# Moving work inside the fourth attention of a fused decoder: bias, residual, statistics, exponentials, two dense steps and the top-p weights

## The reference

```
x = x + tanh(g_xattn[l]) * xattn_l(layernorm(x), ctx)
x = x + tanh(g_ffn[l])   * ffn_l(layernorm(x))
```

```
q = _qdq(x) @ _qdq(wq).T + bq                 # rounded to whole numbers of a scale per token
attn = softmax(q k^T / sqrt(16))              # 16 heads of 16 features, 128 keys per sequence
o = attn v
out = _qdq(o) @ _qdq(wp).T + bp
```

## Time and profile before

| | us |
|---|---|
| median of 3 runs | 1033.53 |
| lowest, highest | 1028.81, 1034.68 |
| the profiled execution | 1037.46 |
| its span | 1035.6 |
| PE busy in the span | 859.2 (83%) |
| DVE, ACT, POOL busy | 677.9, 521.2, 326.0 |

### The profile page before, as it was taken

The page is one execution under the profiler, slowest core; times in us unless marked ns, Lnnn a source line. Parts: engine busy times, 40 slices in busy tenths (PEclk is TensorE's granted clock), DMA queues, the critical chain, the costliest instruction groups (busy, mean ns, idle before and its releaser), DMA issues. The chain is left out here.

```text
span 1035.6 us, 17165 instructions
## 1 busy us (share of the span) xinstructions
PE 859.2 (83%) x6369; PEld 532.9 (51%) x6369; DVE 677.9 (65%) x1402; ACT 521.2 (50%) x840; POOL 326.0 (31%) x267
## 2 busy tenths in 40 slices
PE   5978999776227776797979998778799999999997
PEld 3434665463216564574545554445455556555554
DVE  7985888787817667266336479645778657744343
ACT  4714345445117767336558743455456786533332
POOL 2531343312744555303025662100355333200000
PEclk9988999988659999897879999999999999999999
DMA  8973433310246677331013453111256445433332
GB/s 267 324 254 107 129 107 114 93 33 1 114 151 189 211 225 218 117 113 46 18 32 122 123 170 106 46 32 47 70 174 182 129 129 167 144 105 95 107 94 85
DMA packets 60191, 129.12 MB, mean 125 GB/s; under 512 B 9267, under 2 KB 25025, under 8 KB 60114
## 3 DMA queue, kind: packets, MB, share of 16 engines
q1 hardware_dynamic: 55506, 119.17, 37.4%
q0 software_dynamic: 4608, 8.94, 2.3%
HBM read 83.95 MB, written 48.27 MB: 128 GB/s over the span
## 5 line engine op out<-in xcount | busy, mean ns | idle before, releaser
L1448 PE MATMUL ps<-turned_buf,W 128*128 128x512 f16 x576 | 136.8, 388 | 5.7 <-DVE ctx_sb L2280 1.8
L2280 DVE SCALAR_TENSOR_TENSOR ctx_sb<-ps,ctx_sb 128x512 f32<-128x512 f32 x96 | 66.2, 690 | 111.0 <-PE ps L1448 80.7
L1448 PE MATMUL ps<-turned_buf,wb 128*128 128x512 f16 x576 | 133.5, 382 | 0.0
L2287 DVE TENSOR_TENSOR ctxT<-ctx_sb,ctxT 128x512 f16<-128x512 f32 x96 | 71.4, 744 | 70.7 <-ACT ctxT L1023 70.2
L761 POOL TENSOR_SCALAR W<-W 128x768 f32<-128x768 f32 x32 | 68.6, 2145 | 127.8 <-ACT wb L1035 64.1
L1023 ACT ACTIVATE ctxT<-ctx_sb 128x512 f16<-128x512 f32 x96 | 60.2, 627 | 94.4 <-DVE ctx_sb L2280 94.3
L1015 ACT ACTIVATE ctx_sb<-ps 128x512 f32<-128x512 f32 x96 | 57.3, 597 | 99.3 <-PE ps L1448 99.0
L1448 PEld LDWEIGHTS ps<-turned_buf,W 128*128 128x128 f16 x576 | 56.1, 100 | 69.1 <-issue 8.0
L1391 PE MATMUL ps<-turned_buf,W 128*128 128x512 f16 x360 | 87.3, 396 | 2.5 <-issue 2.5
L1448 PEld LDWEIGHTS ps<-turned_buf,wb 128*128 128x128 f16 x576 | 56.1, 99 | 59.8 <-issue 2.7
L749 POOL DMA_INDIRECT slots<-arena x64 | 62.3, 973 | 68.6 <-ACT arena L1086 56.3
(11 more groups left out here) (411 smaller groups left out, 1719.4 us busy)
## 6 DMA issues: line engine op xcount, KB each, us to landing
W<-in_w SPq DMA_DIRECT2D x77, 384.0 KB, 3.6
seats<-k_st SPq DMA_DIRECT2D x8, 1152.0 KB, 10.9
arena<-seats SPq DMA_DIRECT2D x32, 288.0 KB
kept<-W SPq DMA_DIRECT2D x24, 384.0 KB, 4.0
kept<-wb SPq DMA_DIRECT2D x24, 384.0 KB, 4.2
W<-kept SPq DMA_DIRECT2D x24, 384.0 KB
wb<-kept SPq DMA_DIRECT2D x24, 384.0 KB
wb<-in_w SPq DMA_DIRECT2D x18, 384.0 KB, 11.2
```

The lines of the kernel that those rows point to most:

```text
L1448: last = nc.tensor.matmul(bank(4 + n), w4[k % 4][:, w, n * D + c * P:n * D + (c + 1) * P], x16[:, i, c, half * HALF:(half + 1) * HALF], st ...
L2280: nc.vector.scalar_tensor_tensor(h_g[:, g % 2, :], bank(5), 1.0 / WSCALE, h_s[:, g % 2, :], ALU.mult, ALU.mult).then_inc(sem("gated"), 1)
L2287: nc.vector.tensor_tensor(h_16[:, g % 2, 1, :], h_g[:, g % 2, :], h_16[:, g % 2, 0, :], ALU.subtract)\
```

## The change

- `steps_by`: two dense steps of half 0 come one step later (21 to 22 and 25 to 26), on all four engines. Half 1 has none moved.
- q: the bias goes from step 12 to step 11, directly behind `whole_out` and ahead of step 12's dense work on DVE; `q3_lo` of the first sequence and ACT's `q3_hi` of the first two go from step 13 to step 12.
- ACT: in a step that has both, `p3_exp` comes before `nmT`.
- The residual goes from step 37 to step 36, statistics from 38 to 37, POOL's `inv_sqrt(7)` from 39 to 38, `normalise` from 40 to 39, `turn_half`, `half_x` and `half_x_lo` from 41 to 40, router and `top_p_arg` from 43 to 42. The first `split_hi` of pass 2 goes from step 40 to 39 on ACT.
- `top_p_weights` is cut in three pieces. Those of half 0 come at the end of steps 0, 1 and 2 of half 1, those of half 1 behind the next three dense steps.

```diff
+        THIN_STEPS = (15, 17, 19, 22, 23, 26, 27, 29, 31, 32)
...
-            return min(14 + (s - 13) * 10 // 19, 24) if s < 33 else min(24 + s - 32, 2 * NT2 + 2)
+            return 14 + sum(k <= s for k in THIN_STEPS) if s < 33 else min(24 + s - 32, 2 * NT2 + 2)
...                                                        # POOL
-                    if s == 39:
+                    if s == 38:
                         inv_sqrt(7, halves=(h,))
...                                                        # ACT
-                    if s == 13:
+                    if s == 12:
                         q3_hi(4 * h)
                         q3_hi(4 * h + 1)
...
+                    if s in LESS_AT:
+                        p3_exp(8 * h + LESS_AT.index(s))
                     if s in NM_AT:
                         nmT(4 * h + NM_AT.index(s))
-                    if s in LESS_AT:
-                        p3_exp(8 * h + LESS_AT.index(s))
...
-                    if s in (40, 41) and h == 0:
-                        split_hi(2, s - 40)
-                    if s == 41:
+                    if s == 40:
                         half_x(7, h)
-                top_p_exp(h)
+                    if s in (39, 41) and h == 0:
+                        split_hi(2, s // 41)
+                    if s == 43:
+                        top_p_exp(h)
...                                                        # PE
-                    if s == 41:
+                    if s == 40:
                         turn_half(7, h)
-                    if s == 43:
+                    if s == 42:
                         router(3, (h,), 2)
...                                                        # DVE
                     if s == 11:
                         whole_out(h, 0)
-                    if s == 12:
                         nc.vector.tensor_tensor(a3_y[:, sl, :], a3_y[:, sl, :],
                                                 bq3[:, :].unsqueeze(1).to_broadcast((P, 4, D)), ALU.add).then_inc(sem("q3"), 1)
-                    if s == 13:
+                    if s == 12:
                         q3_lo(4 * h)
...
                     if s == 36:
                         whole_out(h, 1)
-                    if s == 37:
                         dve.wait_ge(sem("x_bias"), h + 1)
                         link(nc.vector.scalar_tensor_tensor(x[:, sl, :], a3_y[:, sl, :], tg[:, 3:4], x[:, sl, :], ALU.mult, ALU.add))
-                    if s == 38:
+                    if s == 37:
                         statistics(7, h)
+                    if s == 39:
+                        normalise(7, h)
                     if s == 40:
-                        normalise(7, h)
-                    if s == 41:
                         half_x_lo(7, h)
-                        if h == 0:
-                            split_lo(2, 1)
-                    if s == 43:
+                    if s == 41 and h == 0:
+                        split_lo(2, 1)
+                    if s == 42:
                         top_p_arg(h)
-                top_p_weights(h)
+                    if s < 3 and h:
+                        top_p_weights(0, s)
             for st in range(steps_by(1, LATE - 1), 2 * NT3):
                 half_step(2, st)
+                if st < steps_by(1, LATE - 1) + 3:
+                    top_p_weights(1, st - steps_by(1, LATE - 1))
```

More of the change, by code:

```diff
@@ L2796, in top_p_arg, with top_p_weights @@
                 nc.vector.tensor_tensor(l_lg[:, sl, :], scores, half_spread(l_s8[:, 0, sl]), ALU.subtract).then_inc(sem("router_arg"), 1)
-            def top_p_weights(h):
+            def top_p_weights(h, part):
                 sl = slice(4 * h, 4 * h + 4)
                 w, total, inv = l_w[:, 1, sl, :], l_s8[:, 1, sl], l_s8[:, 2, sl]
-                dve.wait_ge(sem("router_exp"), 3 + h)
-                link(nc.vector.tensor_reduce(total, l_lg[:, sl, :], AX.X, ALU.add))
-                link(nc.vector.reciprocal(inv, total))
-                link(nc.vector.tensor_tensor(w, l_lg[:, sl, :], half_spread(inv), ALU.mult))
-                half_before(w)
-                link(nc.vector.tensor_tensor(l_eq, l_cmp, w.unsqueeze(2).to_broadcast((P, 4, E3, E3)), ALU.mult))
-                link(nc.vector.tensor_reduce(l_rk, l_eq, AX.X, ALU.add))
-                link(nc.vector.scalar_tensor_tensor(w, l_rk, TOP_P, w, ALU.is_le, ALU.mult))
-                link(nc.vector.tensor_scalar(w, w, tg_ffn[:, 7:8], None, ALU.mult))
+                if part == 0:
+                    dve.wait_ge(sem("router_exp"), 3 + h)
+                    link(nc.vector.tensor_reduce(total, l_lg[:, sl, :], AX.X, ALU.add))
+                    link(nc.vector.reciprocal(inv, total))
+                    link(nc.vector.tensor_tensor(w, l_lg[:, sl, :], half_spread(inv), ALU.mult))
+                if part == 1:
+                    half_before(w)
+                if part == 2:
+                    link(nc.vector.tensor_tensor(l_eq, l_cmp, w.unsqueeze(2).to_broadcast((P, 4, E3, E3)), ALU.mult))
+                    link(nc.vector.tensor_reduce(l_rk, l_eq, AX.X, ALU.add))
+                    link(nc.vector.scalar_tensor_tensor(w, l_rk, TOP_P, w, ALU.is_le, ALU.mult))
+                    link(nc.vector.tensor_scalar(w, w, tg_ffn[:, 7:8], None, ALU.mult))
             for h in range(2):
```

## The result

The changed kernel takes 1016.9 us (median of 4 executions, 1013.12 to 1019.5), the kernel before beside it 1033.03 (4 executions, 1028.81 to 1034.68): a ratio of 0.9851, with a 95% interval of 0.9808 to 0.9894. Forecast was 1020.5, in a range of 1014 to 1029. In a second comparison the same changed kernel came to 0.9886 [0.9842, 0.9929]. So the gain is 12 to 16 us, where 13.0 was forecast, and its terms are to be judged one by one.

The account below looks back on a forecast made before the run. PE's holes without an instruction, mostly in the first half, and the low clock around them were taken as the bound. Terms of 14.2 us, less 1.2, gave 13.0 and a median of 1020.5 us, range 1014 to 1029.

Parts of the forecast that it names:

- The sum of 14.2: Whole kernel: gains of 4.5, 2.9, 2.3, 3.5, 0.4 and 0.6 us added, before a deduction for unseen waits.
- the way to the second gate product of pass 2: Sign: the stretch from 628 us to that product gets some 13.5 us shorter.
- no wait over 1 us before the transposes of x: Sign, end of half 0: PE's wait of 2.72 us there falls to no more than 1 us.
- q, 4.5 forecast: Half 0, turn of q: PE starts 3.05 us earlier, and the clock kept behind it gives another 1.5.
- Exponentials and dense steps: Half 0 attention: exponentials 0.97 us earlier three times, 2.9; two moved half_downs with the clock, 2.3.
- Rival 1: The holes shrink but the clock doesn't come back: 9.3 us are left, 1024.2 us; chance 0.20.
- Rival 3: Slower: new, shorter holes let the clock fall for long in 674 to 708 us, 1044 us; chance 0.04.
- Residual, statistics and normalise: End of half 0: normalise ends earlier and the router starts at 735.2 for 738.76; gain 3.5 us, 2.4 without the clock.
- Top-p in half 0: Start of pass 2: pieces let the first gate product through, new waits of 1.9 and 1.2; gain 0.4 us.
- Second half: Half 1: -0.8 at the bias, 0.5 from exponentials, 0.9 at the tail; gain 0.6 us, bounds -3 and 2.5.
- Rival 2: Second half takes the gain back, paced by a weight's load and ACT's and POOL's split: 1031.5 us; chance 0.10.
- The 1.2 us taken off the sum: Whole kernel: deduction for unseen waits, once more the 0.7 and 0.5 that half_add costs, leaving 13.0 us.

Follow-up runs that it names:

- q_only: The kernel before with only the moves of q (bias, q3_lo, q3_hi one step earlier); ratio 0.9961 to the kernel before, median 1027.31 us.
- q_and_exp: The kernel before with the moves of q and the exponential ahead of the maxima's copy, without the dense steps; ratio 0.9903 to the kernel before.
- exp_only: The kernel before with only the exponential put ahead of the maxima's copy on ACT; ratio 0.9923 to the kernel before.
- early_split: The changed kernel with the first weight split of pass 2 moved to step 37, ahead of POOL's power; ratio 0.987 to the kernel before, 1029.62 us.
- both: The changed kernel with the edits of early_split and half1_order together; ratio 0.9853 to the kernel before, 1026.54 us.
- tail_only: The kernel before with only residual, statistics, power, normalise, transposes, router and first weight splits moved earlier, top-p whole; ratio 0.9985 to the kernel before.
- topp_only: The kernel before with only the top-p weights cut in three pieces; ratio 1.0019 to the kernel before.
- hold_split: The changed kernel with POOL's first weight split of pass 2 held until normalise of half 0 is done; ratio 0.9888 to the kernel before.
- half1_order: The changed kernel with the old order of q and of residual to router put back in half 1 alone; ratio 0.9846 to the kernel before, 1026.63 us.

## Why the prediction was right, and where its terms were not

The time was right, and so was the mechanism for q and the exponentials, where 9.7 us were forecast and 10.4 came. The tail of half 0, top-p and the second half were wrong: 4.5 forecast, -0.2 measured. The sum of 14.2 was 10.3 on the profiles. That the times of the whole kernel still show 12 to 16 us is in part luck, as the last paragraph says. Of the prediction's own signs, the waits and the clock at q, the table load, the waits for L1293 and the wait at the third `turn_max` came as told; the way to the second gate product of pass 2 is 12.1 us shorter, where 13.5 was told, and "no wait over 1 us before the transposes of x" failed.

**q, 4.5 forecast: 4.64.** (Its own figures give 1.22 + 0.43 = 1.65 for the clock, where it wrote 1.5.) The hole of 0.50, the clock at 1.00 behind it, the 0.62 and the 2.75 us are as forecast, in the changed kernel, and A is 11.15 or 11.16 in all eight profiles that have the edit.

**Exponentials and dense steps, 2.9 + 2.3 = 5.2: 5.8** (13.93 + 32.72 against 10.57 + 30.29, from B and C). The swap gives what it was worked out for: the waits of 2.24 are 1.21 (1.27 forecast), and the copy's new place costs nothing that can be seen. The table load has no drain behind it: 653.96 + 1.28 = 655.24, and the exponential starts at 655.26. The rule of the Trainium skill (ScalarE: Activation LUTs, What ACT_TABLE_LOAD costs), which adds a drain of about 1380 ns to each load, did not hold here. The new wait of `turn_max` was forecast at 0.9 and is 0.43, that of scores(4) at 0.5 and is 0.64. The clock's share was larger than the 1.1 taken: of 3.36 us in B, 0.97 is the swap and 0.7 the waits of the step, which leaves 1.7. Rival 1, that the clock doesn't come back, did not come in the changed kernel's two profiles. It came in part where only parts were changed: q_only lost 6.4 us in B and C, more than it won in A, and q_and_exp has 1.6 more there than exp_only. early_split and both lost 1.6 in C with the changed order. Rival 3 (slower by a long fall) named something that happens, but in the order of before: 6.6 us in tail_only, none so long in six profiles with the changed order.

**Residual, statistics and normalise, 3.5, with the 0.4 of top-p 3.9: 1.1** (D, 54.76 against 53.63; apart, 1.6 in tail_only and -0.5 in topp_only). This is the step that failed: "The gate product and then normalise follow, 731.4 to 732.9". The working let normalise take 1.5 us because DVE was free. It did not ask what POOL does in that time, though it had itself moved the first split of pass 2 one step ahead on ACT and counted this as a gain. hold_split shows the cause, 3.27 against 1.37, and its 1.9 us is what is missing at the router, which comes 1.6 us earlier and not 3.5. The other piece was sized well: half_down waits 1.50 us for half_add, 0.86 more than before, where 0.7 was forecast. Most of the 1.1 is the clock's: PE is without an instruction for 9.8 us of D before and 9.5 after, while the transposes went from 2.37 us to 0.78 and 0.76 and the half_down behind them from 2.00 to 1.48. Forecast without the clock was 2.4. hold_split and early_split took the collision away and won nothing in D: the split was then late for PE, or held up another DVE instruction. What a better place for it would give is not shown.

**Top-p in half 0, 0.4 forecast: -0.5.** Forecast were waits of 1.9 and 1.2; measured 1.67 and 2.03, and 0.52 between. The pieces stand in front of DVE's gated product, as foreseen, and with them an L2613 that took 1.83 us and not 0.42, again beside POOL's L765 (720.50 to 722.14).

**Second half, 0.6: -1.3.** E is 1.0 longer: half_down waits 1.06 us for half_add behind the bias, -0.8 forecast. F is 0.8 shorter (0.5 forecast). G is 1.1 longer, where 0.9 shorter was forecast. Here half1_order separates the two edits: the pieces of top-p with the old tail bring 1.1 (161.17 to 160.09; 0.4 in topp_only), the moved tail takes 2.15 back, and 2.25 in tail_only (163.42). Its two waits are the 1.12 for half_lo and 1.51 for half_add. The forecast had no term for the first and put the second at 0.5. In front of both stands a DVE instruction beside a split of POOL: L2021 of 1.37 us (0.17 in half 0), which ends at 856.38, 0.02 after POOL's L765 (854.72 to 856.36), and the half_lo of 1.82 (0.69), beside the L765 of 863.48 to 865.12. In half1_order L2021 takes 0.17, and neither wait is there. So the step that failed in half 0, a DVE instruction priced without POOL beside it, is seen here twice again; no kernel was built to hold these two splits apart. Rival 2, a second half that takes the gain back, is right in kind and small in size, 1.3 of 11.6 us; the waits seen are for half_add and half_lo on DVE, two of them behind an instruction beside POOL's splits, and not for the chain of a weight's load and its splits that it named.

**From 10.3 to 16.1.** The profile of before, with its 71.84 us between the two `whole_turn`s, lay below the mean of the four profiles of that code, 74.1; the six profiles with the changed kernel's order there have 61.4 four times and 63.0 twice. That is some 2 us more than the profiles' difference. The other 3 to 4 are not explained: the interval of the first ratio reaches from 10.9 to 19.8 us, the second comparison gave 11.8, and the start of the stage alone scatters by 20 us. The ratios of the five parts, 0.9961, 0.9923, 0.9936, 0.9985 and 1.0019, multiply to 0.9825; by their intervals this is uncertain by some 0.008 (an estimate), so the times show no loss between the parts and can't rule one out. The 1.2 us taken off the sum for unseen waits were too few for D and the second half (4.7 us under the forecast). What hid this, as far as the runs show, is luck: a kernel before whose clock costs more on the average than in the profile that was worked with, and a first comparison that came out 4 us above the second.

## What to carry to other kernels

When a step is moved on one engine, put its new time beside the list of the engine that can hold it up in memory (DVE and POOL), not only beside its semaphores: four short instructions took more than twice as long here (3.27 us against 1.37) because a split of weights ran beside them. What the clock loses behind PE's holes is priced from several profiles of the same code, since one may be a lucky one. And an order that pays where PE waits (half 0) can cost where PE is full: half1_order, which moves it in the half that has the holes alone, is 3.2 us shorter in E and G.

## What the runs showed of the hardware that was not expected

**DVE and POOL stop each other.** The engines do not meet at semaphores alone. A DVE TENSOR_TENSOR or TENSOR_SCALAR on SBUF alone that started while POOL's L765 (f16 from f32, 768 elements, 1.64 us) runs ended only when L765 had, in all cases listed here: of the four instructions of normalise one took 1.80 us and ended 0.15 after it (the others 0.40 to 0.91), L2021 took 1.25 and 1.37 (0.17), L2613 1.83 (0.42), L2289 1.82 (0.69). BATCH_NORM_AGGREGATE (L2019, 0.15 us each) ran beside it at its usual length. It goes the other way too: L762 of POOL takes 2.13 us, and 3.08 at 754.64, just behind the start of the bias on DVE (754.51 to 755.74). SCALAR_TENSOR_TENSOR from PSUM (L2298, 757.64 to 759.29, 1.65 us) ran beside L765 at its usual length. The Trainium skill (SBUF — State Buffer, SBUF: two separate sides) says that DVE, in a 2-port mode or with two SBUF inputs, and GpSimd take a shared pair of ports under an exclusive lock: the one that starts first has it for the whole instruction and blocks the other. For L765 the trace agrees. For L762 it doesn't quite: L2289, with two SBUF inputs, started at 844.29 in the middle of one (843.11 to 845.24) and took its usual 0.69 us.

**The clock's falls are not reproducible.** B and C of the same instructions took 46.5 and 46.7 us, 48.1 and 53.1. Behind one and the same hole of 2.4 us the clock fell in half1_order and did not in both. A hole of 2 us is not needed either: in early_split the clock fell to 0.50 in 684 to 686 us, behind waits of 1.21 and 0.64, where the same instructions of the changed kernel ran at 1.00. What the runs do show is how much: with the short waits, nothing in four profiles and 1.6 us in two; with those of 2 us and more, up to 6.6 us beyond the best profile of the same code. Why one execution falls and another doesn't stays open.

**A stage of unchanged code scatters more than the change is worth.** The start of the fourth attention lay at 632.73 to 652.65 us in fourteen profiles: at 632.73 to 639.16 in four on one chip, at 641.39 to 652.65 in eight on another.
